# Products of the identity by itself at six waits of the prologue

## The reference

```python
# block 0, a conditioned transformer block; m = silu(cond) @ w_ada + b_ada gives shifts, scales and gates
h = _ln(x) * (1 + sc_msa) + sh_msa
x = x + g_msa * _self_attn(h)          # windows of 128 rows, shifted by 64, 16 heads of 16
h = _ln(x) * (1 + sc_mca) + sh_mca
x = x + g_mca * _topk_cross_attn(h)    # 77 context rows, the 16 highest scores of each row kept
h = _ln(x) * (1 + sc_mlp) + sh_mlp
x = x + g_mlp * _swiglu(h)             # 256 -> 2 x 1024 -> 256
# block 1, experts
nx = _layer_norm(x, gamma, beta)
evidence = softmax(nx @ Wq @ (ctx @ Wk).T / 16) @ (ctx @ Wv)
combined = [nx, evidence, cond]
routed = sum over 3 experts of router_prob * (silu(combined @ e_w1 + e_b1) @ e_w2 + e_b2)
g = sigmoid(silu(combined @ gate_w1 + gate_b1) @ gate_w2 + gate_b2)
return x + g * (routed @ out_w + out_b)
```

## Time and profile before

| | |
|---|---|
| three runs | 1452.98, 1453.32 and 1455.0 us, median 1453.32 us |
| the profiled execution | 1453.46 us |
| its span, from the first to the last instruction | 1451.6 us |
| mean granted clock of TensorE | 0.988 of full |
| busy: PE, DVE, ACT, POOL | 1410.0, 1015.7, 838.9, 427.4 us |
| records on PE | 9701 |

### The profile page before, as it was taken

One profiled execution on the slowest core, in us unless ns is written; L12 is line 12 of the kernel. 1 busy time (PEld: TensorE's weight loads), 2 busy tenths in 40 slices (PEclk: granted clock), 3 DMA queues, 4 the chain that ended last, 5 costly groups with the idle time before them and its releaser, 6 DMA issues.

```text
span 1451.6 us, 29925 instructions
## 1 busy us (share of the span) xinstructions
PE 1410.0 (97%) x9701; PEld 1191.4 (82%) x9701; DVE 1015.7 (70%) x4628; ACT 838.9 (58%) x2555; POOL 427.4 (29%) x613
## 2 busy tenths in 40 slices
PE   7888999999999999999999999999999999999997
PEld 5666888888888888888888788888888878887886
DVE  3485858688695867869595786959587685958642
ACT  3463474846657375665747466574757547574433
POOL 1313132323225232322334232233234313222302
PEclk9889999999999999999999999999999999999999
DMA  7520000010000000010010000000010000000000
GB/s 243 194 73 1 1 1 25 1 34 9 19 30 12 5 2 25 2 34 1 15 42 1 16 2 16 11 16 20 9 47 3 16 1 3 7 2 8 1 3 12
DMA packets 27339, 34.97 MB, mean 24 GB/s; under 512 B 3324, under 2 KB 22448, under 8 KB 26929
## 3 DMA queue, kind: packets, MB, share of 16 engines
q1 hardware_dynamic: 27185, 33.07, 7.3%
HBM read 28.83 MB, written 4.22 MB: 23 GB/s over the span
## 4 chain that ended last, share of the span: by engine, by line
PE 88%; DVE 7%; ACT 2%; issue 2%; SPq 0%; POOL 0%; DMA 0%; DVEq 0%; ACTq 0%; POOLq 0%
PE bank L955 13%; PE bank L910 13%; PE bank L979 11%; PE bank L962 7%; PE bank L919 6%; PE bank L783 6%; PE bank L769 5%; PE bank L842 5%; PE bank L830 4%; PE bank L894 4%; PE bank L822 2%; DVE knocked L2160 2%; PE bank L754 2%; PE bank L740 2%; PE bank L804 1%
## 5 line engine op out<-in xcount | busy, mean ns | idle before, releaser
L910 PE MATMUL bank<-hB,Wm 128*128 128x256 f32 x1024 | 243.5, 384 | 3.6 <-ACT hB L1329 3.6
L910 PEld LDWEIGHTS bank<-hB,Wm 128*128 128x128 f32 x1024 | 191.2, 190 | 35.1 <-issue 8.6
L955 PE MATMUL bank<-nxT,W1nx 128*128 128x256 f32 x896 | 212.2, 383 | 0.0
L1368 ACT ACTIVATE prob<-bank,rmax 128x128 f32<-128x128 f32 x512 | 180.0, 434 | 27.6 <-DVE rmax L2108 27.6
L1719 POOL TENSOR_TENSOR scores<-scores,M 128x308 f32<-128x308 f32 x128 | 94.3, 737 | 321.4 <-DVE knocked L2160 319.0
L1375 ACT ACTIVATE probT<-bank 128x512 f32<-128x512 f32 (+1 forms) x256 | 139.7, 615 | 83.9 <-PE bank L894 77.6
L979 PE MATMUL bank<-W2p,gT 128*128 128x256 f32 x768 | 183.2, 381 | 3.0 <-DVE acc L2239 1.9
L955 PEld LDWEIGHTS bank<-nxT,W1nx 128*128 128x128 f32 x896 | 166.2, 191 | 23.2 <-issue 2.8
L979 PEld LDWEIGHTS bank<-W2p,gT 128*128 128x128 f32 x768 | 141.2, 190 | 23.8 <-issue 2.8
L1407 ACT ACTIVATE tbs<-bank,b1half 128x256 f32<-128x256 f32 x128 | 60.6, 473 | 144.8 <-PE bank L910 104.3
L1423 ACT ACTIVATE tbs<-bank,betaH 128x256 f32<-128x256 f32 x224 | 95.2, 487 | 83.1 <-PE bank L962 83.1
(11 more groups left out here) (228 smaller groups left out, 2699.7 us busy)
## 6 DMA issues: line engine op xcount, KB each, us to landing
Wm_g<-in_L_xcond_w_m_dram SPq DMA_DIRECT2D x4, 1024.0 KB, 5.5
W1ev<-in_L_xcond_e_w_dram SPq DMA_DIRECT2D x6, 512.0 KB, 7.5
x<-in_x_dram SPq DMA_DIRECT2D x16, 128.0 KB, 2.5
x<-in_x_dram SPq DMA_DIRECT2D x32, 64.0 KB, 2.3
Wm<-in_L_xcond_w_m_dram SPq DMA_DIRECT2D x1, 2048.0 KB, 9.2
out_dram<-acc SPq DMA_DIRECT2D x16, 128.0 KB, 1.7
out_dram<-acc SPq DMA_DIRECT2D x32, 64.0 KB, 2.0
batch_rows<-row_store SPq DMA_DIRECT2D x4, 384.0 KB, 3.8
```

The source lines that it names most:

```text
L910: m = pe.matmul(bank_of(name)[:, half * UT:(half + 1) * UT], Wm1[:, k, c:c + P], hB[:, k, :], start=(k == 0), stop=(k == CB - 1))
L955: pe.matmul(bank_of(name)[:, n * UT:(n + 1) * UT], W1nx[:, k, c0 + n * P:c0 + (n + 1) * P], nxT[:, k, :], start=(n == 0 and k == 0), stop= ...
L1368: m = act.activation(prob[:, s, i, :], psum[s][:, i * P:(i + 1) * P], ACT.Exp, bias=rmax[:, t, s * HPS + i:s * HPS + i + 1], accum_out=rsu ...
```

## The change

A helper `idle_products(n)` issues n fp32 matmuls on TensorE with `ident` as weights and as moving operand, into quarters of bank 6 in turn. Each is complete in itself (start and stop), raises no semaphore, and nothing reads what it writes. It is called in six places of TensorE's prologue, with 5, 4, 4, 5, 3 and 5 products. Ahead of the first stands one more `wait_folds(pe)`, since bank 6 is one of the folds' banks; the one at the end of the prologue stays. No other engine's program changes.

```diff
+            def idle_products(n):
+
+                for i in range(n):
+                    pe.matmul(psum[6][:, (i % 4) * P:(i % 4 + 1) * P], ident[:, :], ident[:, :], start=True, stop=True)
 
             def prologue():
...
                 a_turn_probs(1, 2, 1)
                 fold_router_rows()
                 a_turn_probs(1, 3, 1)
+                wait_folds(pe)
+                idle_products(5)
                 a_turn_inverses("r1", "pv", 1)
                 a_values(1, 1)
                 a_turn_picked(0, 0, 0)
...
                 a_turn_picked(1, 1, 0)
                 a_turn_picked(1, 2, 0)
                 a_turn_picked(1, 3, 0)
+                idle_products(4)
                 a_cross_values(1, 0)
                 pe.wait_ge(gatedC, 2)
+                idle_products(4)
                 a_project("xv", oT2, "co", Wco_g, 0)
+                idle_products(5)
                 a_turn_query(1)
+                idle_products(3)
                 a_query(1)
                 turn("ln3", xnB, 0, normed[2], TILES)
                 wait_folds(pe)
...
                 pe.wait_ge(evidence_loaded, 16 * len(evidence_loads))
                 pe.wait_ge(prepared_b, 1)
                 pe.wait_ge(prepared, 1)
+                idle_products(5)
```

## The result

| | before | after |
|---|---|---|
| median of 13 executions each | 1455.0 us | 1451.13 us |
| lowest and highest | 1452.64 and 1457.98 us | 1447.52 and 1452.64 us |
| ratio, with its 95% interval | | 0.9976 [0.9968, 0.9984] |
| span of the profiled execution | 1451.6 us | 1449.4 us |

The change makes the kernel faster by 0.24%, which is 3.5 us (2.3 to 4.7 us by the interval). The two medians are 3.9 us apart; the ratio is the one on record and not their quotient. The forecast was 4.8 us.

The account below looks back on a forecast made before the run. TensorE was taken to bound the kernel behind the prologue, with its clock at half in three prologue stretches. Restoring them gives 1.6 + 1.5 + 1.7 = 4.8 us, so 1453.46 - 4.8 = 1448.7 us; range 1446.0 to 1453.9 us.

Parts of the forecast that it names:

- The bound: Behind the prologue TensorE alone sets the time, busy 1204.29 of 1208.32 us; prologue gains go through to the end.
- The price of a product and the rooms: At six prologue waits, products of 0.22 us each fit rooms of 0.91 to 1.53 us; at full clock they cost nothing.
- the overrun of 0.16 us in the fourth: Ahead of turn ln2, five products take 1.10 us against 0.94 us of room; the later 0.23 us xnB wait absorbs it.
- The rival of products twice as wide: At the six waits, products take 0.43 us and overrun by 4.1 us; 1457.6 us, or 1452.8 with clock held; chance 0.07.
- The gain in the three stretches: Half-clock prologue stretches from 105.03, 118.68 and 128.92 us return to full clock: 1.6 + 1.5 + 1.7 = 4.8 us.
- The rule of a single long gap: A mid-kernel clock fall needs one idle gap longer than any here, so filling changes nothing: 1453.5 us.
- The rival built on it: At the six prologue waits, short waits don't lower the clock, so filling doesn't hold it; 1453.5 us, chance 0.17.
- The other ground for that rival: Identity products may not count as work, nearly all factors being zero; 1453.5 us, within the same chance of 0.17.
- The part-held rival: Of three prologue stretches, two held give 1450.3 us, one gives 1451.8 us; chance 0.17, half at either value.
- the border of 1450.4 us: Whole-kernel time below which the result counts as faster, taking 2.9 us, some 0.2%, as what a measurement can tell.
- The step that was off: In the tail, the 1340.65 to 1347.48 us half-clock stretch stays, worth 3.3 us at most; 2 us allowed in the range.
- The absolute time: Whole kernel: 1448.7 us forecast from a profiled execution of 1453.46 us, with a median of the runs of 1453.32.

Follow-up runs that it names:

- e6_tail: Changed kernel plus two tail groups, 14 products ahead of the last turn ln4 and 10 ahead of the last hidden block; 1447.75 us, 0.9942 of the kernel before.
- e11_after_again: The changed kernel itself, measured and profiled again; 1450.87 us, 0.9973 of the kernel before.
- e12_tail_again: The same kernel as e6_tail, measured again with six executions; 1447.42 us, 0.9941 of the kernel before.
- e9_all: e6_tail plus groups of products at seven earlier prologue waits, into bank 4; 1452.37 us, 0.9976 of the kernel before.
- e1_first_group: Changed kernel with only the first of its six groups kept; 1450.27 us, 0.9961 of the kernel before.
- e14_first_tail_again: Kernel before plus the first prologue group and the two tail groups, a repeat measurement; 1447.88 us, 0.9945 of the kernel before.

## Why the prediction was right, and where it was off

- **The bound.** Right. From L740 to the last ln4, before and after need 1192.16 and 1192.17 us; what the prologue won arrived there undiminished.
- **The price of a product and the rooms.** Right: 0.22 us, six waits filled, and no loss from the overrun of 0.16 us in the fourth, which measured 0.15 us. It was absorbed ahead of the wait for xnB, though, and not by it. Twice the number cost 4.28 us (46.29 less 42.01) where the rooms gave 4.4. The rival of products twice as wide is out.
- **The gain in the three stretches.** Right, and stretch by stretch. Counted from L634, the projection co starts 1.5 us earlier (forecast 1.6), the first hidden block 3.2 us (3.1) and L740 4.81 us (4.8). But the three terms are not independent, as the sum took them: the first group alone brought 3.0 us where its own term was 1.6, the other five 3.3 where theirs were 3.2.
- **The rule of a single long gap.** The rival built on it, that the filling changes nothing, is out: filling gaps of 0.75 to 1.37 us kept the clock full from 99.1 us at the latest to the end of the prologue in all four profiles that have these six groups of 26 products and nothing new ahead of them (after, `e6_tail`, `e11_after_again`, `e12_tail_again`). In `e9_all`, with more groups ahead, a fall came in spite of the six. The other ground for that rival, that products of an identity might not count, is out as well.
- **The part-held rival.** It is out by the trace, not by the total: 1451.13 us lies between its two values, 1450.3 and 1451.8 us, and above the border of 1450.4 us that the prediction drew for a gain. That a gain can be told all the same is due to the 13 executions of each kernel.
- **The step that was off** is the tail. The prediction lets the half-clock stretch from 1340.65 to 1347.48 us stay and puts nothing else for the tail in the sum, only 2 us in the range. That term, put at 0, measured +2.13 us in the profile, 1.49 of it around a fall on the last hidden block. In another profile of the same kernel, `e11_after_again`, the tail took 109.80 us, less than before. So this term is not fixed: 109.8 to 112.8 us for one and the same program. That the change brought the fall is therefore not shown.
- **The absolute time.** 1451.13 us lies in the range, 2.4 us above the forecast. 1.7 us of that is the kernel before itself, whose median over 13 executions is 1455.0 us and not the 1453.32 of the first three. The part ahead of the change spreads most: start to L634 is between 101.0 and 105.7 us in the profiles, and goes with the time at half clock in it, 17.1 us in the shortest and 23.9 in the longest of the versions that leave this part as it is.

What stays open is what sets the place of a fall in one execution. `e1_first_group` and `e14_first_tail_again` have the same prologue and differed in it, and I made no run that controls it.

## What to carry to other kernels

Where one engine bounds a long loop, a chain of short waits in the prologue can cost more in its clock than in idle time. Here cheap work in those waits, with 128 streamed columns and an end before the wait's own, bought 4.8 us back. Size each group from the idle time in the timeline, and look first at what bounds the work that the clock slows: where another engine does, as ahead of L634 in `e9_all`, nothing is won. Compare such versions by parts of their traces and over several executions: a single fall elsewhere, 1.5 us here, is as large as the effect of a group.

## What was not expected of the hardware

- Weight loads of 128 columns with 4 streamed ones, back to back, did not hold the clock: it fell with TensorE's records at 6.54 of 6.70 us.
- A wait of the same length came with a fall or without one: 2.19 us of idle time ahead of the last hidden block had a half-clock stretch of 3.41 us behind it in one profile of the changed kernel, and none in another one and in the kernel before.
- The half-clock stretches inside the kernels lasted 3.4 or 6.8 us, in all twelve traces that are read to the end.
